# Seven stack images at seven of eleven steps, and GpSimd's second-norm power and normalising behind the third selection of their step

## The reference

```
x = x + conv11x11_depthwise(groupnorm(x))          # kernels made from 4 points
t = tokens(x)                                      # 16 x 256 tokens x 96
t = t + attention(layernorm(t))                    # 6 heads of 16, rotary, causal
t = t + ffn(layernorm(t))                          # 96 -> 384 -> 96, sign weights,
                                                   # each product scaled by its largest value over 3 batches
```

## Time and profile before

| | us |
|---|---|
| median of 3 runs (lowest, highest) | 262.39 (262.16, 265.4) |
| the profiled execution | 262.38 |
| its span | 260.5 |
| busy in it: TensorE / VectorE / ScalarE / GpSimd | 221.3 / 203.0 / 135.2 / 112.6 |
| attention steps 1 to 15, about | 113 to 201 |

### The profile page before, as it was taken

The page is one execution under the profiler, slowest core; times in us unless marked ns, Lnnn a source line. Parts: engine busy times, 40 slices in busy tenths (PEclk is TensorE's granted clock), DMA queues, the critical chain, the costliest instruction groups (busy, mean ns, idle before and its releaser), DMA issues.

```text
span 260.5 us, 5344 instructions
## 1 busy us (share of the span) xinstructions
PE 221.3 (85%) x1794; PEld 168.1 (65%) x1794; DVE 203.0 (78%) x530; ACT 135.2 (52%) x308; POOL 112.6 (43%) x143
## 2 busy tenths in 40 slices
PE   6479598999999966698999889698997989999981
PEld 6369587978988943466777777587754635545550
DVE  3857869999999779748898788487486868898965
ACT  1341417765664554565777668276756314426250
POOL 1201154655665453474587443948365135010101
PEclk9759999999999999979999999799998899999995
DMA  3999000567959900025445450000000000101103
GB/s 104 247 337 150 1 0 0 92 132 125 113 109 194 151 2 2 0 70 109 99 96 95 91 94 2 3 3 2 3 0 3 1 0 3 45 1 45 45 3 106
DMA packets 22828, 17.43 MB, mean 67 GB/s; under 512 B 3089, under 2 KB 22162, under 8 KB 22802
## 3 DMA queue, kind: packets, MB, share of 16 engines
q1 hardware_dynamic: 21200, 15.81, 30.3%
q10 hardware_dynamic: 1602, 1.29, 2.2%
HBM read 6.03 MB, written 1.57 MB: 29 GB/s over the span
## 4 chain that ended last, share of the span: by engine, by line
PE 44%; DVE 13%; issue 7%; POOL 3%; ACT 2%; DVEq 0%; POOLq 0%; ACTq 0%
PE bank L1563 8%; PE bank L1733 7%; PE bank L1614 7%; DVE nmax L1073 6%; PE bank L1503 5%; PE bank L1534 3%; PE bank L1515 2%; PE bank L1401 2%; PE bank L1598 1%; PE bank L1582 1%; PE bank L1754 1%; PE bank L1536 1%; PE bank L1548 1%; DVE o_norm L1106 1%; DVE rest_ring L972 1%
## 5 line engine op out<-in xcount | busy, mean ns | idle before, releaser
L1073 DVE TENSOR_REDUCE nmax<-bank 128x3 f32<-128x384 f32 x64 | 45.4, 752 | 15.5 <-PE bank L1503 15.5
L732 ACT ACTIVATE pt_ring<-bank 128x384 f32<-128x384 f32 x96 | 42.1, 492 | 14.6 <-PE bank L1536 13.6
L1401 PE MATMUL bank<-xs_ring,toep 128*128 128x192 f32 x256 | 47.3, 334 | 1.2 <-DVE xs_ring L941 1.2
L530 POOL TENSOR_SCALAR_AFFINE_SELECT pt_ring<-pt_ring 128x512 f32<-128x512 f32 x48 | 31.1, 651 | 33.0 <-ACT pt_ring L732 33.0
L1401 PEld LDWEIGHTS bank<-xs_ring,toep 128*128 128x128 f32 x256 | 43.1, 195 | 3.3 <-issue 2.1
L487 POOL TENSOR_TENSOR parts<-rest_ring,parts 96x512 bf16<-96x512 f32 x16 | 20.8, 1300 | 22.1 <-ACT parts L664 22.1
L1503 PE MATMUL bank<-stack 128*128 128x128 bf16 (+1 forms) x288 | 23.2, 225 | 4.4 <-DVE nmax L1073 2.8
L1534 PE MATMUL bank<-stack 97*128 97x256 bf16 x96 | 23.7, 281 | 1.3 <-ACT pt_ring L732 1.3
L1503 PEld LDWEIGHTS bank<-stack 128*128 128x128 bf16 (+1 forms) x288 | 18.0, 101 | 10.1 <-issue 6.5
L1733 PE MATMUL bank<-parts,w_b 128*96 128x512 f32 (+1 forms) x60 | 23.1, 492 | 1.5 <-issue 1.3
L1563 PE MATMUL bank<-pt_ring,v_ring 128*32 128x128 f32 (+1 forms) x448 | 22.8, 330 | 1.4 <-POOL pt_ring L530 1.4
(11 more groups left out here) (145 smaller groups left out, 431.1 us busy)
## 6 DMA issues: line engine op xcount, KB each, us to landing
stack<-parts SPq DMA_DIRECT2D x96, 96.0 KB, 3.6
tok<-in_x_tok SPq DMA_DIRECT2D x4, 384.0 KB, 12.1
stack<-in_const SPq DMA_DIRECT2D x1, 1152.0 KB, 18.6
out<-xs_ring SPq DMA_DIRECT2D x4, 288.0 KB, 2.6
stack<-in_x ACTq DMA_DIRECT2D x2, 384.0 KB, 8.5
stack<-in_const SPq DMA_DIRECT2D x1, 576.0 KB, 5.9
stack<-nmax_t SPq DMA_DIRECT2D x32, 1.5 KB
stack<-in_x SPq DMA_DIRECT2D x2, 192.0 KB, 4.3
```

The source lines that it names most:

```text
L530: nc.gpsimd.affine_select(out=v, in_=v, compare_op=ALU.is_ge, fill=0.0, base=0, pattern=[[0, 2], [0, 2], [1, P]], channel_multiplier=-1).t ...
L732: nc.scalar.activation(pt_ring[:, b % 2, h, :], bank[:, 3 + h % 2, 0:T + P], ACT.Exp, scale=float(HD) ** -0.5).then_inc(s_exp, 1)
L1073: last = nc.vector.tensor_reduce(nmax[:, b % 2, k:k + 3], bank[:, 0:3, first:first + (t + 1) * P], op=ALU.max, axis=AX.X, negate=True)
L1401: last = nc.tensor.matmul(dst, w, xs_ring[:, s, p, k].rearrange("p b c -> p (b c)"), start=(part == 0 and p == 0), stop=(part == 1 and p = ...
```

## The change

On SyncE images 9 to 15 stand behind the maxima of batches 2, 4, 5, 7, 8, 10 and 11 in place of 2 to 8. On GpSimd `select(n, 2)` stands directly behind `select(n, 1)` (and behind `sines` in step 1) in every step, ahead of `second_rstd(0)` and `second_norm`, and `second_norm(1)` is in step 11 in place of step 12. No instruction is added or removed.

```diff
+IMAGE_AT = (2, 4, 5, 7, 8, 10, 11)
...
             for b in range(2, B):
                 max_row(b)
-                if b + RING - 2 < B:
-                    stack_image(b + RING - 2)
+                if b in IMAGE_AT:
+                    stack_image(RING + IMAGE_AT.index(b))
...
                 select(n, 1)
                 if n == 1:
                     sines(0, PAIRS - 1, 1)
+                select(n, 2)
                 if n == 9:
                     second_rstd(0)
                 if n == 10:
                     second_norm(0)
-                if n == 12:
+                if n == 11:
                     second_norm(1)
-                select(n, 2)
                 if n == 14:
                     second_rstd(1)
```

## The result

The changed kernel is faster by 1.55%: ratio to the kernel before 0.9845, 95% interval 0.9811 to 0.9880, which is 4.1 us of 263. The medians of 21 runs each are 261.90 us (258.26 to 267.7) and 263.47 us (261.73 to 267.14). Single executions of one and the same kernel spread over several us, so the ratio compares only those within 1.5% of the fastest of their kernel, 20 of 21 before and 11 of 21 after.

The account below looks back on a forecast made before the run. TensorE was taken to bound the attention steps, with GpSimd's power delaying batch 9's value product. Idle time −1.48 and low clock −1.39, images 0, sum to −2.87: from 262.38 to 259.5 us, range 257.7 to 261.8.

Parts of the forecast that it names:

- What bounds: Attention steps: TensorE and what VectorE gives back set them; GpSimd sets the end only at step 9's power, 2.27 us.
- Part 1, the idle time: Step 9: third selection ahead of the power lets TensorE's value product of batch 9 start 1.48 us earlier.
- PV(9): Start of TensorE's value product of batch 9 (PV(n) for batch n); forecast at 164.41 in place of 165.89.
- The rule that I weighed against the change: GpSimd contends with VectorE's two-SBUF-input instructions; moved pairs could end 1.3 us later each, cover shrinking to 0.3, sum unchanged.
- Part 1, the clock: After batch 9's product TensorE stays at 2.4 GHz; next distance 4.89 in place of 6.28, 1.39 us less.
- Part 1, the covers: Third selections of batches 10 and 11 end 1.2 us before their products want them; moving the second pair costs 0.
- Part 2: Spacing the image DMAs on SyncE's queue: earlier rows gain 0, the last image is not late; 0 in all.
- hidden wait: Possible TensorE wait for row DMAs behind SyncE's full queue in the attention steps; forecast as none, gain 0.
- the 3.95 of the forecast: SyncE's queue: issuing an image's six DMAs takes 3.95 us; for the last image, about 161.1 to 165.1.
- The sum: Whole kernel: −1.48 − 1.39 = −2.87 us, from 262.38 to 259.5, 1.1% less.
- the rest moves as a block: Everything behind step 10 depends on TensorE and VectorE alone and shifts earlier together, later stages unchanged in length.
- The rival of a later stretch that goes away: Stage from 195 on: its low-clock stretch at 200 may vanish too, priced 1.39, giving 258.1 us; chance 0.12.

Follow-up runs that it names:

- e4: Kernel before with the third selection moved ahead of the power in step 9 alone, norm pairs and images as before; ratio to before 1.0008.
- e3: Changed kernel with GpSimd's old order restored, so only the images are spaced out; ratio to before 1.0041.
- e2: Changed kernel with the images back as before, so only GpSimd's new order stays; ratio to before 0.9925.
- e10: Kernel before with only VectorE's second-norm statistics moved ahead of its second maxima in step 9; batch 8 to 9 product distance 5.31 us, from 7.20.
- e12: Changed kernel with VectorE's statistics and weight preparation in its idle time, but images back behind maxima 2 to 8; ratio to before 0.9855.
- e5: Changed kernel with image 15 behind the maximum of batch 13 instead of 11; batch 10 to 11 product distance 10.71 us, from 4.89.
- the second comparison: Changed kernel, unedited, compared with the kernel before once more; ratio 0.9915 (0.9854 to 0.9975).

## Why the prediction was right, and where it missed

**What bounds.** Right. The wait of TensorE for the third selection was the place, and its removal is the gain that all profiles of the new order share.

**Part 1, the idle time.** PV(9) was to come 1.48 us earlier; it came 1.21 (7.20 to 5.99). The step that failed is the assumption that moving the selection forward leaves VectorE's statistics and normalising where they were. The rule that I weighed against the change was looked at from GpSimd's side alone, and there nothing happened (its pairs stayed at 1.15). What was lost was lost on VectorE: the mean, an operation with two SBUF inputs, began beside the selection and took 0.26 longer, and the product came 0.27 later than forecast. The Trainium skill, GPSIMD Engine Reference, section Key points, names just such instructions, and the trace agrees, with 0.43 against 0.17.

**Part 1, the clock.** I took 1.39 as a full gain. The low clock costs 1.4 where it falls, and it falls in three of four profiles of the old order. On average that is about 1.0 us, an estimate from four profiles, so the term was oversized for a mean and right for the execution that I read. Step 10 and 11 were 4.89 each as forecast, and the sum over the stage 2.60 against 2.87.

**Part 1, the covers.** 1.2 us was forecast for the third selections of batches 10 and 11; after the change they end at 173.73 and 178.63 and their products start at 174.94 and 179.83: 1.2 each. The prediction priced only the pair that leaves step 12, at nothing, and gave none for moving the one of step 10. e4 gives it: with that pair left in front, 0.4 us of the gain is lost again. The pair had had its cover before only from the very wait that the change removes.

**Part 2.** Worth 0 in this change: e3 has no gain and e2 loses none. But the prediction's "I find no room for any" hidden wait was too sure. The same order has a wait of 0.48 us in one profile (e10), when one issue took 2.04 us, and the earlier trace rows had shown one of 2.24; e12 shows where a full queue leads. The last image's issues took 5.07 us in the changed kernel, not the 3.95 of the forecast, and ended at 171.60, about 1.2 us later in the step than forecast. Its cover was 4.4 all the same, as worked out with e5.

**The sum and the measured gain.** 2.87 was forecast. 4.1 was measured in the first comparison (3.2 to 5.0 by its interval), 2.2 in the second (0.9915) and 2.0 with the selection alone. The profiles account for 1.2 in each and 1.4 more in most, 2.2 in the mean, which agrees with the second comparison, though its own interval is wide. No distance in the profiles is shorter beyond what is listed, so no stage shows the surplus of the first. The record of single executions shows where it lies. The changed kernel did the same both times: its shortest took 258.26 and 258.43 us. The kernel before did not: none of its 21 executions in the first comparison was under 261.7, and 7 of its 35 in the second took 259.7 to 260.7. By the medians of all executions the change gains 1.6 and 1.5 us. So the surplus comes from which executions of the kernel before were met, and 4.1 is no measure of the change. That the forecast of 2.87 lies between 1.5 and 4.1 is in part luck; the evidence for its terms is the stage, 2.60.

The assumption that the rest moves as a block holds for the instructions: PV(11) to PV(15) is 24.29 or 24.05 in both kernels. It doesn't hold for the clock behind it. From PV(15) to the end the kernel before took 58.1 to 59.3 us and the changed one 58.0 and 61.7, with a low stretch from about 203 to 213 in the latter. The rival of a later stretch that goes away is not borne out as an effect of the change: the changed kernel has it in one profile and not in the other, and so has the kernel before.

## What to carry to other kernels

In an engine's queue, put what another engine waits for ahead of what only has a far reader, and when you do so look at what stood one place further: its cover may have been the wait that you remove. A queue that is just full (5.65 us of issues in steps of 5.3 to 6) may show no wait on the page and take back part of the gain of the next improvement. Work that only has to be done some time belongs in front of an operation that is waiting anyway, not behind it: for VectorE here it gave 0.85 us for the statistics and 2.2 us for the weights.

## What the runs showed of the hardware that I had not expected

An operation of VectorE with two SBUF inputs can be held up by a GpSimd instruction that began before it, until that one ends: the 0.43 us above, and, larger, a product of 128 by 384 that takes 0.55 us alone and 2.39 us beside GpSimd's selections and its own product of two tensors in step 1. VectorE's timeline of the changed kernel has both lengths, for two batches:

```profile
118.21 2.39 DVE L966 TENSOR_TENSOR rc_ring<-qk_ring,cst 128x384 f32<-128x384 f32 x1
...
124.52 0.55 DVE L966 TENSOR_TENSOR rc_ring<-qk_ring,cst 128x384 f32<-128x384 f32 x1
```

And this is what GpSimd did beside the first:

```profile
117.99 1.22 POOL L532 TENSOR_SCALAR_AFFINE_SELECT pt_ring<-pt_ring 128x512 f32<-128x512 f32 x2
119.19 0.99 POOL L482 TENSOR_TENSOR rs_ring<-qk_ring,cst 128x384 f32<-128x384 f32 x1
120.29 0.80 POOL L532 TENSOR_SCALAR_AFFINE_SELECT pt_ring<-pt_ring 128x512 f32<-128x512 f32 x1
```

The product began 0.22 us behind the start of the selections and was done 0.4 us behind the end of GpSimd's own product: it was held up by three instructions in a row. Seven other profiles of this study, one of the kernel before among them, have that product at 2.35 to 2.39 us as well, each time 0.21 to 0.25 us behind the start of a selection. The remaining six have it at 0.55 to 0.58. In those it began when the selection before it was over or had 0.17 us or less to go, and the next selection is the longer one, with 0.91 to 0.95 us in place of 0.64. The first profile of before has it so:

```profile
114.59 0.55 DVE L964 TENSOR_TENSOR rc_ring<-qk_ring,cst 128x384 f32<-128x384 f32 x1
```

```profile
114.72 0.91 POOL L530 TENSOR_SCALAR_AFFINE_SELECT pt_ring<-pt_ring 128x512 f32<-128x512 f32 x1 [0.33 <-ACT pt_ring L732]
```

So the one that began second pays. The earlier trace rows is the second case, with the selection behind and 0.98 us long, and the mean of step 9 is the first. No experiment here moved one of these instructions alone to set who begins; the rule is read from the order in the traces.

TensorE's granted clock can fall to 1.2 GHz behind a wait of 1.4 us, and stay up behind the same wait in another execution (e3). A fall cost 1.4 us in 9-10 and in 1-2. Such stretches lie at several places, and with them the same code comes out at different times: PV(0) lies between 113.63 and 117.57 in the 14 profiles, and from PV(15) to the end the changed kernel took 58.0 and 61.7. What sets their place was not tried.
